# RWKV-7 block on one core: a second ring of four banks in the first half of a section, small roots as powers on GpSimd, and a new order of the steps

## The chip, the cores and the metric

The kernel runs on one core of a Trainium2 chip. The metric is the device time of one execution in microseconds (us), as the median of several runs. The core has five engines that run side by side: TensorE (PE in the profile; PEld is its weight load), VectorE (DVE), ScalarE (ACT), GpSimd (POOL) and SyncE (SP), which here only issues transfers. They meet through semaphores only.

## What is computed

The input x is 2 x 4096 tokens of 256 channels, fp32. After a layer norm it goes through two branches, whose product is added to x:

```python
xn = _layernorm(x)
s = _L0_attn_ref(xn, ...)          # RWKV-7 time mixing, 4 heads of 64
g = _silu(_L0_ffn_ref(xn, ...))    # down(silu(gate(x)) * up(x)), 256 -> 768 -> 256
x = x + s * g
```

In the time mixing, each token is mixed with the one before it by four sets of weights made from a small tanh layer (mix0 to mix3, for wa, k, rg and v). From the mixed inputs come the receptance r, the key k, the value v, the decay w, the rates a and ma, the gate g and the normed key kk. Then runs a recurrence over the tokens of each head:

```python
S = S * dt[:, :, None, :] + sa[..., None] * bt[:, :, None, :] + vt[..., None] * kt[:, :, None, :]
y = jnp.einsum('bhij,bhj->bhi', S, rt)
```

with `sa = S at`, a = -kk, b = kk * a. Its output goes through a group norm over each head, (yh - mu) * rsqrt(var + EPS), gets a bonus term, is multiplied by g and projected by w_output.

## The kernel before

The 4096 tokens of both batches are cut into 16 tiles t of 256 tokens (512 columns with two batches). The recurrence is worked in blocks of 32 tokens: within a block by triangular matrices, from block to block by a state ST, in eight steps c of a tile.

Every engine has its own program, made of the same streams, each a generator that does one step per `yield`. In a *section* up to four tiles are in work at once: L is the input norm of tile i+1; F (mixing), D (decays), K (keys), R (receptance), V (values), E (update) and X (pairs) are the front part of tile i; N (the feed-forward part) and B (back, the recurrence) are for tile i-1; O (output) is for tile i-2. There are 15 sections that hold front and back together.

The order of the steps on an engine is a string, ORDER, with one letter for each step; walk() takes the next step of the stream that the letter names. An engine works its instructions strictly in this order. Written out with step names, PE's first part of a section before is:

```
gate00 gate01 up00 mix0 up01 yT0 yT1 gate02 gate03 up02 up03 out0 mix1 gate04
lora gate05 k0 out1 z gh v0 k1 hk v1 r0 r1 band corner kk vT0 up04 up05 values0
state0 rn vT1 u0 g0 ...
```

gate and up are halves of the feed-forward's products (4 matmul instructions each, since fp32 takes two passes), down and ffn its last product, xT, yT and vT transposes, band and corner the last two products of the inverse of a 32 x 32 triangle, whose 16 x 16 parts VectorE inverts in the steps inv0 to inv14 and flip. values, state, u, s and y are the steps of the recurrence, half, matrix and KT those of the pairs.

PSUM has eight banks. Four of them (`bank`) are a Ring: room() gives the next one and makes PE wait until its last tile has been read. Nearly all products of PE outside the recurrence take one. The other four (`chunk_banks`, also seen as `spare_bank`) belong to the recurrence; in the first half of a section mix0 (L381) and then the first parts of z, na and nma (L397, L400, L406) use them at fixed places, with the signals mix_made, z_made and rates_made. back() has PE wait, ahead of values0, until ScalarE has taken z, na and nma of the next tile.

Lines that matter below: L356 is the matmul of project(), for lora, k, hk, gh, r, v and mixin; L386 mix1; L422 kk and mk; L455 vT; L506 gate and up; L516 down; L535 band and L543 corner; L559 values, L568 outputs, L584 state, L598 u, L612 s; L625 yT; L634 out. On ScalarE L648 is the square root of the input norm and L900 that of the group norm, each followed by a reciprocal on VectorE (L929, L1182); L701 copies k, L820 and L823 are the decays' Exp and Ln, L839 is the Silu of the gate, L680 and L684 the sigmoids, L865 takes y out, L871 band. On VectorE L962 is the mixing, L969 the decays' n, L986 the fl steps, L996 kk. On GpSimd L1246 adds the mixed parts to x, L1272 is mkz, L1282 e3, L1305 fades the state, L1236 moves the last token of a tile.

SyncE's program after a tile's pairs are done is a chain: store and reload the matrices for the inverse, load the residual (`Y<-in_x`), store the inverse, reload it for band, and load its parts into TT ahead of values0.

Of the kernel before, what the change touches and what calls it, by code (L numbers as in the profile page):

```python
# [16 lines left out]
H, N = 4, 64  # L17
# [30 lines left out]
for _n, _w in (("ident", 128), ("bd", 128), ("center", 128), ("am0", 256), ("ti", HL * HL)):  # L48
# [4 lines left out]
ORDER = {"pe": ("NNNFNOONNNNOFNFNKOFRVKKVRRBBKVNNBBKVBVBBVBBBBBNBBBNBBBNBBNBBNEBNNNBBNNBBNNBNBBXXBBNXXXBXBBNBBLBNBBXX"  # L53
            "BBLXXXX"),
         "act": ("ONNNFKFFFOOFFRFDKVKDVBRRBKKKVVBEBKBBBKVBXXBBVDBVBBVNNXBLBBNXBNBBXXLBXBBLLBXBBNXBBLXX"),
         "dve": ("BOFNOONBBBOBFFFFFFFBOBBBBBBBBBBBDDDDDKKDDNKDKDBBBXEBLBEXBXBEXBXEXENXXBXXLXBNXXBXXXXXNBXXXBXXXXXBXXXL"
             "BLXXXBXBX"),
         "pool": ("FFFFFFFFDBFEXEBKBXBBBBBL")}
# [54 lines left out]
def program(nc, d):  # L113
    with ExitStack() as ctx:
# [13 lines left out]
        eps = sb("eps", [128, 4])  # L128
# [41 lines left out]
        qpad = [sb(f"qpad{i}", [128, QC, NJ, 2, 2, BL]) for i in range(2)]  # L170
# [12 lines left out]
        SF = sb("SF", [128, B, NH, N])  # L183
        rhs = sb("rhs", [128, 2, 128])
# [17 lines left out]
        ring = Ring(bank, [semaphore(f"bank_full{i}") for i in range(NB)])  # L202

# [8 lines left out]
        mix_made, z_made, rates_made = signal("mix_made", 4), signal("z_made", NH), signal("rates_made", 2)  # L212
# [36 lines left out]
        NSET = 13  # L249
# [95 lines left out]
        def pe_program():  # L345
# [28 lines left out]
            def mixing(t):  # L374
                pe.wait_ge(*mixh_ready(t))
                if t >= 2:
                    pe.wait_ge(*y_out(t - 2))
                    pe.wait_ge(*st_ready(t - 2))
                for n in range(4):
                    f = MIX[n][0]  # L380
                    pe.matmul(spare_bank[n], w2[32 * f:32 * f + 32, 0:128], small[32 * f:32 * f + 32, :], start=True, stop=True).then_inc(*mix_made.up)  # L381
# [7 lines left out]
                o = room((t, "lora"), lora_ready(t))  # L389
                pe.wait_ge(*moved(t, 2))  # L390
                project(o[0:112, :], wa1, xwa).then_inc(*ring.fill((t, "lora")))
                yield "lora"
                pe.wait_ge(*lora_ready(t))
                pe.wait_ge(*mixed(t, 7))
                two = [room((t, "na"), na_ready(t)), room((t, "nma"), nma_ready(t))]
                for g in range(NH):
                    pe.matmul(spare_bank[g], wa2[32 * g:32 * g + 32, 128 * g:128 * g + 128], sml2[32 * g:32 * g + 32, :],  # L397
                              start=True, stop=False).then_inc(*z_part.up)
                for n, p0 in enumerate((64, 96)):
                    pe.matmul(spare_bank[2 + n], wa2[p0:p0 + 16, 0:128], sml2[p0:p0 + 16, :], start=True, stop=True).then_inc(*rates_made.up)  # L400
# [1087 lines left out]
```

## Time and profile before

| | us |
|---|---|
| median of 3 runs | 1805.75 (1799.24 to 1811.61) |
| the profiled execution | 1809.13 |
| its span, first to last instruction | 1807.7 |
| mean granted TensorE clock | 0.941 of 2.4 GHz |
| DMA engines, mean | 32 GB/s |

The profiled execution lies within the runs. All durations and gaps that the prediction uses are from it; 1.4 us lie outside its span. A page of the profile gives busy time by engine and by group of instructions; a busy PE is not PE at its peak, since matmuls overlap and their ends are modelled. The granted clock is either 1 or 0.5 (2.4 or 1.2 GHz) and a number between is a mean over a stretch. A wait is put down to the one that came last.

### The profile page before, as it was taken

How to read it: one execution, taken by the hardware profiler on the slowest of the kernel's cores; microseconds unless marked ns; L12 is line 12 of the kernel's file. 1: busy time of each engine (PE TensorE's matmuls, PEld its weight loads, DVE VectorE, ACT ScalarE, POOL GpSimd, SP SyncE). 2: the span in 40 equal slices, each digit the busy share in tenths (PEclk: the TensorE clock that was granted, in tenths of full speed). 3: DMA queues.
4: the chain of work that ended last, by engine and by line, in shares of the span. 5: the costliest groups of instructions: out<-in, count | busy, mean ns of one | idle time of the engine just before them, and what ended most of it. 6: DMA issues, size and time to landing. Idle time of an engine off the chain costs nothing.

```text
span 1807.7 us, 47903 instructions
## 1 busy us (share of the span) xinstructions
PE 1625.3 (90%) x20224; PEld 1116.4 (62%) x20224; DVE 1234.1 (68%) x2608; ACT 1207.0 (67%) x2047; POOL 480.0 (27%) x388
## 2 busy tenths in 40 slices
PE   1679999999998999999899999999999999999966
PEld 0255757667575766757576675757667575765745
DVE  3476777677676777767677676777777676776713
ACT  1838758584875858587584958768585875849512
POOL 0414132241313224141332414132241413324000
PEclk9879999999998999999899999999999999999968
DMA  3011020211202021110201112030211203011110
GB/s 132 12 17 31 9 51 14 50 22 30 42 8 51 14 46 25 30 42 6 54 15 40 31 30 42 3 58 14 45 26 30 42 3 58 14 40 19 35 25 25
DMA packets 251430, 57.83 MB, mean 32 GB/s; under 512 B 223696, under 2 KB 250704, under 8 KB 251088
## 3 DMA queue, kind: packets, MB, share of 16 engines
q1 hardware_dynamic: 241936, 41.95, 12.3%
q10 hardware_dynamic: 9280, 12.81, 2.0%
q8 instruction: 160, 2.62, 0.6%
q14 instruction: 54, 0.44, 0.1%
HBM read 36.38 MB, written 18.35 MB: 30 GB/s over the span
## 4 chain that ended last, share of the span: by engine, by line
PE 77%; SPq 6%; DVE 5%; ACT 4%; DMA 4%; issue 3%; POOL 0%; DVEq 0%; ACTq 0%
PE bank L356 16%; PE bank L506 16%; PE bank L516 10%; PE bank L481 7%; DMA Y<-in_x 3%; PE chunk L612 3%; PE chunk L584 3%; PE chunk L559 3%; PE bank L455 3%; PE chunk L568 2%; PE bank L468 2%; PE bank L634 2%; PE bank L461 2%; PE chunk L598 2%; SPq L1342 1%
## 5 line engine op out<-in xcount | busy, mean ns | idle before, releaser
L506 PE MATMUL bank<-xT,wu 128*128 128x256 f32 x768 | 219.8, 423 | 0.0
L506 PE MATMUL bank<-xT,wg 128*128 128x256 f32 x768 | 202.1, 400 | 18.3 <-DVE KS L962 18.3
L1305 POOL TENSOR_TENSOR SF<-ST,CT 128x256 f32<-128x256 f32 x128 | 97.4, 761 | 450.4 <-DVE ST L1168 450.4
L839 ACT ACTIVATE sg<-bank 128x512 f32<-128x512 f32 x96 | 57.1, 595 | 228.9 <-PE bank L506 228.5
L516 PE MATMUL bank<-wd,hT 128*128 128x256 f32 x768 | 186.5, 393 | 0.0
L1246 POOL TENSOR_TENSOR big<-KS,xT 128x512 f32<-128x512 f32 x64 | 75.2, 1197 | 407.1 <-DVE KS L962 407.1
L506 PEld LDWEIGHTS bank<-xT,wg 128*128 128x128 f32 x768 | 142.8, 196 | 60.1 <-DVE KS L962 30.7
L356 PE MATMUL bank<-big,W 128*128 128x512 f32 (+1 forms) x320 | 167.2, 657 | 13.1 <-POOL big L1246 6.5
L506 PEld LDWEIGHTS bank<-xT,wu 128*128 128x128 f32 x768 | 151.3, 209 | 36.6 <-issue 11.4
L516 PEld LDWEIGHTS bank<-wd,hT 128*128 128x128 f32 x768 | 143.2, 193 | 22.0
L356 PE MATMUL bank<-KS,W 128*128 128x512 f32 x320 | 144.2, 597 | 0.0
L1163 DVE COPY VU<-chunk 32x256 f32<-32x256 f32 x128 | 53.4, 417 | 126.4 <-PE chunk L598 125.9
L481 PE MATMUL bank<-qpad,KS 128*64 128x32 f32 x4096 | 134.0, 225 | 4.8 <-DVE KE L1100 4.5
L865 ACT ACTIVATE Y<-chunk 32x256 f32<-32x256 f32 x256 | 96.3, 376 | 62.4 <-PE chunk L568 58.3
L481 PEld LDWEIGHTS bank<-qpad,KS 128*64 128x64 f32 x4096 | 127.0, 140 | 14.3 <-issue 11.8
L969 DVE SCALAR_TENSOR_TENSOR gT<-big,gT 128x1024 f32<-128x1024 f32 x16 | 39.1, 2445 | 118.5 <-ACT big L823 118.5
L356 PEld LDWEIGHTS bank<-big,W 128*128 128x128 f32 (+1 forms) x320 | 62.8, 204 | 84.3 <-issue 61.0
L356 PEld LDWEIGHTS bank<-KS,W 128*128 128x128 f32 x320 | 59.5, 190 | 81.2 <-issue 81.2
L1128 DVE TENSOR_TENSOR hT<-sg,bank 128x512 f32<-128x512 f32 x96 | 65.9, 686 | 52.3 <-PE bank L506 46.0
L1168 DVE TENSOR_TENSOR ST<-SF,chunk 128x256 f32<-128x256 f32 x128 | 53.8, 420 | 61.9 <-PE chunk L612 60.7
L882 ACT ACTIVATE rhs<-chunk 96x256 f32<-96x256 f32 x128 | 48.2, 376 | 71.0 <-PE chunk L584 69.1
L802 ACT ACTIVATE qpad<-big 64x256 f32<-64x256 f32 x256 | 92.0, 406 | 1.6
(161 smaller groups left out, 3559.9 us busy)
## 6 DMA issues: line engine op xcount, KB each, us to landing
smalls<-in_x SPq DMA_DIRECT2D x32, 256.0 KB, 3.0
Y<-in_x SPq DMA_DIRECT2D x32, 256.0 KB, 3.7
out<-fsil ACTq DMA_DIRECT2D x32, 256.0 KB, 2.2
scrA<-AM SPq DMA_DIRECT2D x64, 64.0 KB, 1.9
hat<-scrB SPq DMA_DIRECT2D x32, 128.0 KB, 3.3
hat<-scrF SPq DMA_DIRECT2D x32, 128.0 KB, 3.1
KE<-scrA SPq DMA_DIRECT2D x64, 32.0 KB, 2.3
scrT<-KE SPq DMA_DIRECT2D x16, 128.0 KB, 1.7
```

The source lines that it names most:

```text
L356: m = pe.matmul(o, weights[:, h, :], x[:, h, :], start=(h == 0), stop=(h == NH - 1))
L455: q = pe.matmul(o[:, 128 * n:128 * n + 128], bv[t % 2][:, h, 128 * n:128 * n + 128], center, start=True, stop=True)
L481: q = pe.matmul(oc[:, :, BL * j:BL * j + BL], K[:, 2 * n + b, 64 * j:64 * j + 64], Q[:, 2 * n + b, j, :, :, :].rearrange("p a b e -> p (a ...
L506: q = pe.matmul(o[:, TT_ * n2:TT_ * n2 + TT_], w[:, h, 128 * (n + n2):128 * (n + n2) + 128], x_now[:, h], start=(h == 0), stop=(h == NH - 1))
L516: q = pe.matmul(o[:, 256 * m:256 * m + 256], hT[:, n, 128 * m:128 * m + 128], wd[:, n, :], start=(n == 0), stop=(n == NF - 1))
L559: pe.matmul(RY[g:g + 64, b, 64 * h2:64 * h2 + 64], A[64 * b:64 * b + 32, c, 64 * h:64 * h + 64], V[64 * b:64 * b + 32, c, 64 * h:64 * h + ...
L802: i = act.activation(Q[p0:p0 + 64, :, :, hh, x, :], own[p0:p0 + 64, qs], ACT.Copy)
L839: act.activation(sg[:, :], ring.tile(key)[:, :], ACT.Silu).then_inc(*sg_ready.up)
L865: i = act.activation(by_batch, RY[64 * x + 32:64 * x + 64, :, :].rearrange("p b (g n) -> p b g n", g=NH), ACT.Copy)
L1128: i = dve.tensor_tensor(hT[:, n:n + 2, :], sg[:, :].rearrange("p (n c) -> p n c", n=2), ring.tile(key)[:, :].rearrange("p (n c) -> p n c", ...
L1246: pool.tensor_tensor(columns(dst[:, h, :]), columns(w[:, h, :]), x_now_of(par, h), ALU.add).then_inc(*moved.up)
L1305: pool.tensor_tensor(SF[:, :, :, :], ST[:, :, :, :], fade[:, c].unsqueeze(3).to_broadcast([128, B, NH, N]), ALU.mult).then_inc(*faded.up)
```

## The change

**A second ring.** A Ring `spare` is put over the four banks of the recurrence, with a semaphore for each bank. early_room() takes the next one and waits for its reader, and for the recurrence of two tiles before. mix0's four products, lora, the two parts of z, na0, nma0, k0, k1, hk, gh, r0, r1, v0 and v1 go there; the first ring keeps the rest. The signals mix_made, z_made and rates_made go.

```diff
         ring = Ring(bank, [semaphore(f"bank_full{i}") for i in range(NB)])
+        spare = Ring(spare_bank, [semaphore(f"spare_full{i}") for i in range(len(spare_bank))])
...
+            def early_room(t, key, emptied):
+
+                o, before = spare.take(key, emptied)
+                if before:
+                    pe.wait_ge(*before)
+                if t >= 2:
+                    pe.wait_ge(*y_out(t - 2))
+                    pe.wait_ge(*st_ready(t - 2))
+                return o
...
                 pe.wait_ge(*lora_ready(t))
-                pe.wait_ge(*mixed(t, 7))
+                four = [early_room(t, (t, "z", g), z_ready(t, g + 1)) for g in range(NH)]
+                four += [early_room(t, (t, name), taken(t, 1)) for name, taken in (("na0", na_ready), ("nma0", nma_ready))]
...
                 for h in range(NH):
-                    o = room((t, "k", h), k_ready(t, h + 1))
-                    project(o[:, :], wk[:, :, 128 * h:128 * h + 128], xk).then_inc(*ring.fill((t, "k", h)))
+                    o = early_room(t, (t, "k", h), k_ready(t, h + 1))
+                    project(o, wk[:, :, 128 * h:128 * h + 128], xk).then_inc(*spare.fill((t, "k", h)))
...
                 pe.wait_ge(*t_loaded(t))
                 if t + 1 < NT:
-                    for taken in (z_ready, na_ready, nma_ready):
-                        pe.wait_ge(*taken(t + 1, 2 if taken is z_ready else 1))
+                    for taken in (z_ready, k_ready, hk_ready, gh_ready, r_ready, v_ready):
+                        pe.wait_ge(*taken(t + 1))
+                    for taken in (na_ready, nma_ready):
+                        pe.wait_ge(*taken(t + 1, 1))
```

With four tiles in the ring, the tenth product (nma0) takes the bank that k0 took, k1 that of z0, hk that of z1, gh that of na0, v0 that of nma0, v1 that of k1, r0 that of hk and r1 that of gh.

**Roots.** The square root on ScalarE and the reciprocal on VectorE become an add of the epsilon and a power of -0.5, both on GpSimd, for the input norm (128x4) and the group norm (128x16). The 1/N of the group norm moves into the Square on ScalarE (a scale). They stand in GpSimd's program after state4 and after state7.

```diff
-                act.activation(rstd[:, :], mv[:, :, 1], ACT.Sqrt, bias=eps[:, 0:1]).then_inc(*x_std.up)
...
-                act.activation(st2[:, :], st2[:, :], ACT.Sqrt, bias=eps[:, 1:2], scale=1.0 / N).then_inc(*y_std.up)
...
+                pool.wait_ge(*y_var(t))
+                pool.tensor_scalar(st2[:, :], st2[:, :], GN_EPS, None, ALU.add).then_inc(*y_std.up)
+                pool.wait_ge(*y_std(t))
+                pool.tensor_tensor(st2[:, :], st2[:, :], minus_half.to_broadcast([128, NM * H]), ALU.pow).then_inc(*y_inv.up)
+                yield "root"
```

**The order.** All four strings are new. Written out, PE's section is now:

```
gate00 gate01 yT0 up00 yT1 up01 gate02 gate03 out0 up02 up03 mix0 mix1 gate04 gate05
lora k0 z out1 k1 hk gh v0 kk v1 r0 r1 rn up04 band up05 corner vT0 down0(2 halves)
gate10 values0 state0 gate11 up10 u0 values1 up11 gate12 s0 gate13 state1 vT1 y0 u1 rk
values2 s1 g0 state2 y1 u2 values3 s2 g1 state3 up12 y2 u3 up13 values4 s3 half0 state4
matrix0 y3 u4 gate14 values5 s4 gate15 state5 y4 u5 KT0 values6 s5 up14 state6 half1 y5
u6 matrix1 values7 s6 up15 state7 KT1 xT y6 u7 half2 matrix2 s7 y7 down1 KT2 half3
matrix3 down1 mixin KT3
```

ScalarE from lora to u0: `lora k0 gate04 na0 nma0 z0 z1 na1 nma1 exp k1 hk ln mk0 mk1 gh sqk v0 em r0 band r1 v1 (two output transfers) corner rn_ln rn vT00 vT0 er state0 ek EF es u0`. VectorE: `groupnorm yT0 yT1 up00 unit inv0 inv1 out0 up02 inv2 mix00 ... mix31 inv3 ... inv10 out1 inv11 ... inv14 flip kk0 n nd kk1 cs2 cs4 cs8 rn0 rn1 up04 fl3 fl2 fl1 dm k fl0 b rk qa u0 s0 qa0 ...`. GpSimd: `state0 mix00 ... mix31 mixa zero mkz e3 kem kk qr state1 ... state4 root state5 state6 x0 state7 root`. SyncE's order is the same as before.

**Small.** The constants eps become two columns, 1 and -0.5; two memsets fewer at the start; qpad is declared later, so it lies at another address.

## Rows read from the trace of the kernel before

**Rows 1.** The page's first part: engine, busy us (share of the span), instructions
```profile
PE 1625.3 (90%) x20224; PEld 1116.4 (62%) x20224; DVE 1234.1 (68%) x2608; ACT 1207.0 (67%) x2047; POOL 480.0 (27%) x388
```

**Rows 2.** Busy time by stretch: from:to, length, busy us, PEclk, DMA share, GB/s
```profile
230.00:336.00 106.00, 100.64 (x1272) 69.71 (x1271) 77.50 (x164) 75.46 (x129) 30.09 (x24) 0.97 0.16 33
...
972.00:1078.00 106.00, 99.59 (x1266) 68.29 (x1265) 76.54 (x162) 75.45 (x128) 30.02 (x24) 0.97 0.15 31
...
1502.00:1608.00 106.00, 100.83 (x1264) 69.33 (x1264) 76.29 (x163) 75.43 (x128) 30.07 (x24) 0.95 0.15 30
```

**Rows 3.** The chain that ended last, in order of time: start, us, what
```profile
245.87 12.21 PE bank L356 x28
...
1624.19 12.21 PE bank L356 x28
```

**Rows 4.** Waits of PE: what waited <- for what: total us, times, longest
```profile
PE bank L506 <- DVE KS L962: 18.3, 15, 2.2
PE bank L386 <- DVE fsil L1205: 14.6, 14, 1.4
...
PE bank L455 <- DVE KS L996: 14.0, 16, 1.9
...
PE bank L543 <- ACT hat L871: 12.6, 16, 0.8
```

**Rows 5.** PE alone by stretches of 1 us: length, busy (x), PEclk, DMA share, GB/s
```profile
1109.00:1110.00 1.00, 1.00 (x8) 0.50 0.27 28
...
1115.00:1116.00 1.00, 1.00 (x5) 0.60 0.00 0
...
1293.00:1294.00 1.00, 1.00 (x4) 0.65 0.00 0
```

**Rows 6.** Timeline of PE: start us, us, instruction, count
```profile
1076.23 1.89 PE L506 MATMUL bank<-xT,wu 128*128 128x256 f32 x8
...
1113.57 3.00 PE L506 MATMUL bank<-xT,wu 128*128 128x256 f32 x8
```

**Rows 7.** Timeline of ScalarE about the group norm's root
```profile
1069.72 1.28 ACT L900 ACT_TABLE_LOAD   x1
1071.01 0.31 ACT L900 ACTIVATE st<-st,eps 128x16 f32<-128x16 f32 x1
1071.34 1.28 ACT L839 ACT_TABLE_LOAD   x1
```

**Rows 8.** Groups of instructions: count, busy us, mean ns, idle before
```profile
L839 ACT ACT_TABLE_LOAD x31 | 39.8, 1283 | 0.6
...
L1236 POOL COPY xT<-xT 128x4 f32<-128x4 f32 x16 | 5.9, 371 | 7.1 <-DVE AM L1223 7.1
```

**Rows 9.** Timelines of GpSimd (L1246, L1272, L1282) and VectorE (L969, L986)
```profile
1086.80 4.63 POOL L1246 TENSOR_TENSOR KS<-KS,xT 128x512 f32<-128x512 f32 x4
...
1112.63 2.36 POOL L1272 TENSOR_TENSOR big<-big,gT 128x1024 f32<-128x1024 f32 x1 [6.89 <-ACT big L712]
1114.95 1.89 POOL L1282 TENSOR_TENSOR big<-big 128x1024 f32<-128x1024 f32 x1
...
1104.31 2.51 DVE L969 SCALAR_TENSOR_TENSOR gT<-big,gT 128x1024 f32<-128x1024 f32 x1 [6.71 <-ACT big L823]
...
1112.65 4.31 DVE L986 TENSOR_TENSOR KS<-KS,big 128x32 f32<-128x32 f32 x2
```

**Rows 10.** Timeline of ScalarE: k0's copy, then a sigmoid, load and Exp
```profile
1089.32 0.60 ACT L701 ACTIVATE KB<-bank 128x512 f32<-128x512 f32 x1
...
1096.65 0.74 ACT L684 ACTIVATE big<-bank,nvec 128x512 f32<-128x512 f32 x1
1097.41 1.28 ACT L820 ACT_TABLE_LOAD   x1
1098.70 1.06 ACT L820 ACTIVATE big<-big 128x1024 f32<-128x1024 f32 x1
```

**Rows 11.** Timeline of PE at the end, with the idle time before
```profile
1794.22 1.97 PE L625 MATMUL bank<-con,Y 128*128 128x128 f32 x8 [5.14 <-DVE Y L1184]
```

More of the change, by code:

```diff
@@ L183, in program @@
         SF = sb("SF", [128, B, NH, N])
+        qpad = [sb(f"qpad{i}", [128, QC, NJ, 2, 2, BL]) for i in range(2)]
         rhs = sb("rhs", [128, 2, 128])
@@ L375, in mixing @@
                 pe.wait_ge(*mixh_ready(t))
[L376 to L379, printed above, removed]
+                four = [early_room(t, (t, "mix0", n), mixed(t, 2 * n + 1)) for n in range(4)]
+                for n, o in enumerate(four):
                     f = MIX[n][0]
-                    pe.matmul(spare_bank[n], w2[32 * f:32 * f + 32, 0:128], small[32 * f:32 * f + 32, :], start=True, stop=True).then_inc(*mix_made.up)
+                    pe.matmul(o, w2[32 * f:32 * f + 32, 0:128], small[32 * f:32 * f + 32, :], start=True, stop=True).then_inc(*spare.fill((t, "mix0", n)))
                 yield "mix0"
@@ L728, in receptance @@
                 key = (t, "gh")
-                act.wait_ge(*ring.full(key))
+                act.wait_ge(*spare.full(key))
                 act.wait_ge(*ring.full((t, "nma")))
-                act.wait_ge(*z_made(t))
-                act.activation(sml2[:, :], ring.tile(key)[:, :], ACT.Tanh).then_inc(*gh_ready.up)
+                for g in range(NH):
+                    act.wait_ge(*spare.full((t, "z", g)))
+                act.activation(sml2[:, :], spare.tile(key), ACT.Tanh).then_inc(*gh_ready.up)
                 yield "gh"
-                act.wait_ge(*ring.full((t, "r", NH - 1)))
+                act.wait_ge(*spare.full((t, "r", NH - 1)))
                 for h in range(NH):
-                    act.activation(rT[:, h, :], ring.tile((t, "r", h))[:, :], ACT.Copy).then_inc(*r_ready.up)
+                    act.activation(rT[:, h, :], spare.tile((t, "r", h)), ACT.Copy).then_inc(*r_ready.up)
                     yield f"r{h}"
@@ L744, in value @@
                     key = (t, "v", h)
-                    act.wait_ge(*ring.full(key))
-                    act.activation(bv[par][:, h, :], ring.tile(key)[:, :], ACT.Copy).then_inc(*v_ready.up)
+                    act.wait_ge(*spare.full(key))
+                    act.activation(bv[par][:, h, :], spare.tile(key), ACT.Copy).then_inc(*v_ready.up)
                     yield f"v{h}"
@@ L957, in mixing @@
                         dve.wait_ge(*xx_ready(t, h + 1))
-                    if h == 0:
-                        dve.wait_ge(*mix_made(t))
-                    else:
-                        dve.wait_ge(*ring.full((t, "mix", n)))
-                    dve.scalar_tensor_tensor(out=w[:, h, :], in0=ring.tile((t, "mix", n))[:, :] if h else spare_bank[n], scalar=v(maa, h),
+                    dve.wait_ge(*(ring.full((t, "mix", n)) if h else spare.full((t, "mix0", n))))
+                    dve.scalar_tensor_tensor(out=w[:, h, :], in0=ring.tile((t, "mix", n))[:, :] if h else spare.tile((t, "mix0", n)), scalar=v(maa, h),
                                              in1=xx[:, h, :], op0=ALU.add, op1=ALU.mult).then_inc(*mixed.up)
@@ L1212, in dve_program @@
             n_set = 0
-            for level, col in ((LN_EPS, 0), (GN_EPS, 1), (1.0, 2), (0.0, 3)):
-                dve.memset(eps[:, col:col + 1], level).then_inc(s_set, 1)
+            for level, col in ((1.0, 0), (-0.5, 1)):
+                dve.memset(one[:, col:col + 1], level).then_inc(s_set, 1)
                 n_set += 1
@@ L1252, in decays @@
             def decays(t):
-                pool.wait_ge(*ring.full((t, "v", NH - 1)))
+                pool.wait_ge(*spare.full((t, "v", NH - 1)))
                 pool.memset(FL[:, :, :], 0.0).then_inc(*fl_zero.up)
```

95 lines of the change are left out of this document (46 added, 49 removed).

## Prediction

> **What bounds the kernel now.** I read the page's busy times first: TensorE (PE) is busy 90% of the span, ScalarE 67%, GpSimd 27% [rows 1]. PE's matmuls are the same before and after the change, so the question is what lies between them and at what clock they run. The stretches by section come next [rows 2]. There are thirteen stretches of 106 us between 230 and 1608 us, each as long as a full section; the first, the one with the least work and the last are shown. PE is busy 99.6 to 101.0 us in them, 100.5 in the mean, so 5.5 us are idle, and the mean granted clock is 0.97 in five and 0.95 in eight, 0.958 over all. So PE is at its lower level, 1.2 GHz, for (1 - 0.958) / 0.5 = 8% of the time, 8.9 us of 106. Of these some 1.5 us are idle anyway, and half of the rest, 3.7 us, is what the low clock costs. The chain of what ended last gives the period: its longest piece, 28 matmuls of L356 in a row, stands in it fourteen times, first at 245.87 and last at 1624.19 us, so a section takes 1378.32 / 13 = 106.0 us [rows 3]. A section at full clock and without idle time would take 106.0 - 5.5 - 3.7 = 96.8 us. All that a new order can win is in these 9.2 us, plus the ends of the program.
>
> The waits say who causes the idle time [rows 4]. The gates of L506 wait for the mixing on VectorE (18.3 us in all), mix1 (L386) for a bank that out0 holds (14.6), vT for kk on VectorE (14.0), the corner matmuls (L543) for band's copy on ScalarE (12.6). Nearly all stand in the first half of a section, where every projection takes a bank from one ring of four, while the recurrence's own four banks lie nearly empty. The clock falls just there: at 1109 us, after band, corner and two waits between them, until 1115 us, and in other sections also at 1293 us, behind mix1 [rows 5]. PE was then busy with short, narrow matmuls and gaps. Eight L506 matmuls take 1.89 us at full and 3.00 us at the low clock [rows 6].
>
> **The change, part by part.**
>
> *Roots on GpSimd.* ScalarE loses two square roots a section. The group norm's costs a table load of 1.28 us, and the Silu behind it another [rows 7]; the input norm's root costs a load too. There are 207 loads in the run, 13 a section, of 1283 ns each (L839's 31 stand in [rows 8]). In the new ScalarE order I count 8 changes of table a section: Sigmoid, Exp, Ln, Sigmoid, Exp, Ln, Exp, Silu. That is 6.4 us, and 0.6 us of roots, of some 75 us that ScalarE is busy. VectorE loses two reciprocals of 0.2 us. GpSimd gains four tiny instructions; power isn't in the trace. Its nearest row is a copy of 128x4, 371 ns [rows 8]; as upper bound I take 2.36 us, a 128x1024 add [rows 9]. The group norm's pair stands behind variance, which by the sum below ends 5.7 us before the section does, and yT0 is due 1.7 us after its start. So 0.8 to 4.7 us are hidden; I take 0.8. The input norm's pair has some 3 us of cover. Worth to the path: nothing in itself; it shortens ScalarE's queue.
>
> A table load starts 0.02 us after the last Sigmoid's end, and the Exp 0.01 us after the load [rows 10]. The Trainium skill (ScalarE: Activation LUTs, What ACT_TABLE_LOAD costs) adds a drain of about 1380 ns to each load; by that five loads fewer would be an estimated 13.3 us of ScalarE time, by the rows 6.4. The rows decide.
>
> *The second ring.* mix0, lora, z, na0, nma0, k, hk, gh, r and v move to the recurrence's four banks. PE copies nothing more; it waits for other readers. In return values0 waits until ScalarE has taken all of z, k, hk, gh, r and v of the next tile; in the new order all are taken some 7 us earlier.
>
> *The new order.* I follow a section, time 0 at gate00, with steps at full clock: half a gate or up 0.86 us, projections and out 1.73, half a down 2.79, a recurrence step 0.39, pairs of a quarter 1.99. The dense start (gates, yT, out0, ups) takes 9.5 us with every operand in time, mix0 and mix1 2.0 more: 11.5. Then come these stalls of PE:
> - gate04 needs the bank of mix01, which VectorE frees at 12.3: 0.9 us (before 18.3 / 15 = 1.2).
> - gate04, gate05, lora run to 15.9. k0 needs xk, the fourth add of GpSimd: four of them take 4.63 us [rows 9], from 11.5 to 16.1: 0.3.
> - z needs nma0's bank, which k0 holds; ScalarE copies k0 in 0.60 us [rows 10] plus two handovers: 0.75. This wait is new.
> - k1 needs z0's bank, behind a table load, na0, nma0 and z0 on ScalarE: 0.3.
> - r1 needs gh's bank. ScalarE has to pass, from 18.6 on, z1, na1, nma1, Exp, k1, hk, Ln and the mk pair, with four loads: gh is done at 34.8, PE there at 34.3: 0.5.
> - rn needs the squares of kk. VectorE takes kk1 behind the decays' n, 2.51 us [rows 9], and nd: kk1 ends at 35.5, the squares at 37.5, PE is there at 36.6: 1.05.
> - corner, vT1, u2, s0 and s2: 0.1 to 0.4 each, 1.05 together.
>
> Sum 4.85 us in the first 65 us. In the rest the recurrence has less dense work between its steps; I take 0.9 us, between nothing and the 6.3 of the last rival below. Idle 5.75 us, slightly more than before.
>
> One thing supports itself thinly: on ScalarE everything from k0's copy to u0 (18 to 55 us) is one chain with hardly a gap, and u0's copy ends at 54.9 us, when PE arrives at 55.0. VectorE's u0 stands behind b, rk and qa, which wait for kk on GpSimd, done at 50.3; it ends at 54.3. No slack is left there.
>
> VectorE's inverse steps inv3 to inv10 now lie beside GpSimd's adds. The row shows what happens then: two fl additions took 4.31 us together, until GpSimd's two instructions of 2.36 and 1.89 us were over [rows 9]. The Trainium skill (SBUF — State Buffer, SBUF: two separate sides) calls the pair of ports that both share an exclusive lock, and the trace agrees. Sixteen instructions of 0.24 us would by the row end at 23.7 us instead of 20.8; out1 comes at 22.6 and what follows needs the flip only by 39.5 us less the 7.5 us of loads. By row or rule, this costs PE nothing.
>
> *Clock.* Where the low clock came before, PE now mixes dense steps in: gate halves between band and corner, two downs behind them, vT after them. The narrow stretches are shorter, but z with its wait (3 us) and rn, band, corner with theirs remain. Bounds: 0, or 3.7 us as before. I take 1.0, since part of a low stretch would fall into waits for ScalarE.
>
> Period: the same matmuls, 96.8 by the difference above; my sum from the steps is 94.3 us, and before it lacked some 1.9 us of small overheads (drains ahead of a wait, mostly), 96.2. With 96.2 + 5.75 + 1.0 = 103.0 us a section wins 3.0 us, times 15 = 45 us.
>
> *Ends.* In the last sections PE idles on the recurrence's tail: 5.14 us in front of the last yT [rows 11]. The new order puts all of down1 (5.6 us) behind y7 and down0 in front of values0, where PE waited for loads, and one table load leaves the last chain. 8 us, between 0 and 14. The prologue I take as unchanged, as I do qpad's new address and two memsets fewer.
>
> Sum: 1807.7 - 45 - 8 = 1755 us of span, against an execution that took 1809.1 with a median of 1805.75: the median to expect is **1753 us**.
>
> **The rivals.**
> - *The clock never falls* and idle time stays at 4.6: period 101, 15 x 5 + 8 = 83 us, 1723. For it: dense steps stand in every narrow stretch. Against it: z.
> - *The clock falls once a section as before*: 3 us instead of 1, less shadow: period 105 to 104.9, 15 + 8 = 23 us, 1783. For it: PE has as much idle time as before.
> - *The second ring only moves the waits.* ScalarE's chain from k0 to u0 is 2 us longer than I sum, at no slack: period 105 plus a low stretch, near 106, and of the ends' 8 us some 6 remain: 1800.
> - *The recurrence becomes the bound* (the slower side). Steps 1 to 7 are now only 3.3 to 6 us apart on PE, with copies on VectorE and ScalarE behind instructions of up to 1.2 us. If each of the seven waits 0.9 us, that is 6.3 us, 5.4 more than counted: 15 x (103.0 + 5.4 - 106.0) = 36 us over before with nothing won at the ends, 1842. It decides from some 0.55 us a step on, where 3.0 + 0.9 us are used up by seven. For it: less dense work is left there to cover a copy. Against it: ScalarE has fewer table loads to run between two steps.
>
> **How the numbers follow.** Forecast (1740 to 1770) 0.35, clock never falls 0.22, falls as before 0.20, waits only moved 0.12, recurrence bound 0.11. The range 1715 to 1800 leaves out the last and the lower part of the second. A measurement tells about 1% from no change, 18 us: faster is below 1788. The first three lie there, 0.77 less a rest of the third: 0.76. Same 0.13, slower 0.11.
>
> **What would show it.** Right: 8 table loads a section; a wait of z for ScalarE's k0; a wait of rn; yT0 without wait; idle time of 5 to 6 us, mean clock 0.98 or more. Wrong: a clock of 0.95; waits of u, s or state steps over 0.5 us each; a GpSimd power of over 4 us, which would show before groupnorm.

## The result and the profile after

Measured beside the kernel before, medians of four runs each (for before, the three runs told above and one more):

| kernel | median us | lowest to highest | ratio to before | 95% interval |
|---|---|---|---|---|
| before | 1808.34 | 1799.24 to 1811.61 | 1 | |
| after | 1724.39 | 1710.04 to 1724.95 | 0.9524 | 0.9463 to 0.9586 |

The profiled execution of after took 1724.95 us, its span 1723.5 (before 1807.7). The span lost 84.2 us, 4.7%. The forecast was 53 us.

The page's first part after, to lay beside [rows 1]:

```profile
PE 1580.1 (92%) x20224; PEld 1088.6 (63%) x20224; DVE 1256.4 (73%) x2574; ACT 1099.9 (64%) x1937; POOL 538.1 (31%) x452
```

PE works the same 20224 matmuls in 45 us less busy time: their clock has risen, the mean granted clock of the execution from 0.941 to 0.973. The other 39 us of the span are idle time of PE. ScalarE has lost 107 us of work, GpSimd has gained 58.

Where along the span did it go? The band matmuls (L535 before, L546 after) mark each section. First, last but one and last of each kernel, timelines of PE, start and length in us:

```profile
154.45 1.15 PE L535 MATMUL bank<-hat 64*64 64x64 f32 x32
...
1636.33 1.15 PE L535 MATMUL bank<-hat 64*64 64x64 f32 x32
...
1729.27 1.97 PE L535 MATMUL bank<-hat 64*64 64x64 f32 x32 [14.11 <-issue]
```

```profile
150.60 1.15 PE L546 MATMUL bank<-hat 64*64 64x64 f32 x32
...
1561.73 1.15 PE L546 MATMUL bank<-hat 64*64 64x64 f32 x32
...
1644.94 1.97 PE L546 MATMUL bank<-hat 64*64 64x64 f32 x32 [11.56 <-issue]
```

The front won 3.85 us. Fourteen intervals won 1481.88 - 1411.13 = 70.75, that is 5.05 us each (from 105.85 to 100.80 us). The last interval won 9.73 (92.94 to 83.21), and the tail behind the last band lost 0.2 (78.4 to 78.6).

What a full section is made of shows best in stretches cut at the section's own marks (the start of down's 24 matmuls of L527 in the chain, of L356's 28 before). Columns: from:to, length, then busy us of PE, PEld, DVE, ACT, POOL, granted clock, DMA share, GB/s. Two sections of before, one with the least and one with a typical amount of low clock:

```profile
989.49:1093.23 103.74, 97.94 (x1266) 67.75 (x1265) 76.64 (x163) 75.45 (x129) 30.02 (x24) 0.98 0.15 32
1197.97:1304.00 106.03, 100.88 (x1265) 69.19 (x1265) 76.61 (x163) 75.43 (x129) 29.97 (x24) 0.95 0.15 31
```

Two of after:

```profile
1159.13:1259.44 100.31, 96.26 (x1265) 66.50 (x1265) 78.06 (x161) 68.57 (x122) 33.46 (x28) 1.00 0.16 33
1259.44:1361.60 102.16, 97.91 (x1266) 67.17 (x1265) 77.91 (x161) 68.70 (x122) 34.18 (x28) 0.98 0.16 32
```

A section's matmuls at full clock take 96.3 us: the first row of after shows it, with 1265 matmuls at clock 1.00. What PE is busy above that is the price of the low clock. Before, it was 1.7 us in the first of the two rows, 4.6 in the second, up to 5.8 in others (102.1 us busy), and by the mean of [rows 2] 100.5 - 96.3 = 4.2. After, ten of the thirteen sections between 255 and 1566 us last 100.3 to 100.6 us, 100.4 in the mean, and the last three 102.0 to 102.5, as in the second row, with 1.65 us of low clock: 0.4 in the mean. Over all fourteen intervals from band to band, the mean busy time of PE went from 100.3 to 96.7 us and its idle time from 5.6 to 4.1. So of the 5.05 us, 3.6 are clock and 1.4 idle time. (Fifteen times 3.6 is 54 us, more than the 45 that PE's busy time lost in all: the tail gives some back, as will be seen.)

Where the clock still falls, it is behind z, one of the places named in advance. PE alone by stretches of 1 us, in the section that starts at 1315 us, where z had waited 1.44 us until 1335.44:

```profile
1336.00:1337.00 1.00, 1.00 (x14) 0.95 0.05 16
1337.00:1338.00 1.00, 1.00 (x8) 0.50 0.00 0
...
1340.00:1341.00 1.00, 1.00 (x6) 0.84 0.00 0
```

The waits of PE after, against [rows 4]:

```profile
PE chunk L407 <- ACT KB L711: 20.1, 16, 1.4
PE bank L517 <- DVE KS L965: 13.1, 15, 0.9
...
PE bank L500 <- ACT sg L850: 9.2, 14, 0.7
PE bank L441 <- ACT KS L728: 8.5, 16, 0.6
```

L407 is z waiting for ScalarE's copy of k0 (new, 1.26 us a section), L517 gate04 (0.87), L500 KT3 (0.66), L441 rn (0.56). The waits of mix1, vT and corner that stood in every section are gone.

### The profile page after: what moved, and what is told of

The parts are those of the page before. It is cut to its first block, busy times and chain, and to the rows that moved or that the text cites. A ratio compares the mean times of both kernels' runs of the same rounds, so it can differ in the third digit from the quotient of the medians.

```text
span 1723.5 us, 48139 instructions
## 1 busy us (share of the span) xinstructions
PE 1580.1 (92%) x20224; PEld 1088.6 (63%) x20224; DVE 1256.4 (73%) x2574; ACT 1099.9 (64%) x1937; POOL 538.1 (31%) x452
## 4 chain that ended last, share of the span: by engine, by line
PE 73%; DVE 9%; ACT 7%; issue 4%; POOL 4%; SPq 2%; DMA 2%; DVEq 0%; ACTq 0%; POOLq 0%
PE bank L517 18%; PE bank L527 9%; PE chunk L367 9%; PE bank L492 6%; POOL big L1252 3%; PE bank L647 3%; PE chunk L597 3%; PE chunk L625 3%; PE chunk L572 3%; PE bank L466 2%; PE bank L479 2%; PE bank L472 2%; PE chunk L581 2%; PE bank L500 2%; ACT Y L876 2%
## 5 line engine op out<-in xcount | busy, mean ns | idle before, releaser
L517 PE MATMUL bank<-xT,wg 128*128 128x256 f32 x768 | 199.5, 392 | 13.7 <-DVE KS L965 13.1
L517 PE MATMUL bank<-xT,wu 128*128 128x256 f32 x768 | 210.8, 400 | 0.0
L1311 POOL TENSOR_TENSOR SF<-ST,CT 128x256 f32<-128x256 f32 x128 | 81.9, 639 | 329.3 <-DVE ST L1171 329.2
L527 PE MATMUL bank<-wd,hT 128*128 128x256 f32 x768 | 180.7, 390 | 0.0
L517 PEld LDWEIGHTS bank<-xT,wg 128*128 128x128 f32 x768 | 138.5, 190 | 46.6 <-DVE KS L965 25.5
L527 PEld LDWEIGHTS bank<-wd,hT 128*128 128x128 f32 x768 | 144.9, 194 | 20.3
L517 PEld LDWEIGHTS bank<-xT,wu 128*128 128x128 f32 x768 | 136.4, 192 | 32.6 <-issue 12.2
L492 PE MATMUL bank<-qpad,KS 128*64 128x32 f32 x4096 | 139.8, 225 | 8.2 <-DVE KE L1103 8.2
L367 PE MATMUL chunk<-KS,W 128*128 128x512 f32 x320 | 144.6, 598 | 0.0
L367 PE MATMUL chunk<-big,W 128*112 128x512 f32 (+1 forms) x256 | 119.5, 600 | 6.7 <-ACT gT L702 3.0
L367 PEld LDWEIGHTS chunk<-KS,W 128*128 128x128 f32 x320 | 59.2, 190 | 81.9 <-issue 75.0
L850 ACT ACTIVATE sg<-bank 128x512 f32<-128x512 f32 x96 | 57.2, 595 | 82.4 <-DVE hT L1131 58.2
L682 ACT ACTIVATE smalls<-chunk 64x512 f32<-64x512 f32 x16 | 9.5, 591 | 148.7 <-PE chunk L367 148.7
L1152 DVE SCALAR_TENSOR_TENSOR KE<-KE 128x15 f32<-128x15 f32 (+7 forms) x240 | 89.9, 375 | 9.5 <-DMA KE<-scrA 1.7
```

Source lines behind the costliest of these rows:

```text
L492: q = pe.matmul(oc[:, :, BL * j:BL * j + BL], K[:, 2 * n + b, 64 * j:64 * j + 64], Q[:, 2 * n + b, j, :, :, :].rearrange("p a b e -> p (a ...
L517: q = pe.matmul(o[:, TT_ * n2:TT_ * n2 + TT_], w[:, h, 128 * (n + n2):128 * (n + n2) + 128], x_now[:, h], start=(h == 0), stop=(h == NH - 1))
L527: q = pe.matmul(o[:, 256 * m:256 * m + 256], hT[:, n, 128 * m:128 * m + 128], wd[:, n, :], start=(n == 0), stop=(n == NF - 1))
L850: act.activation(sg[:, :], ring.tile(key)[:, :], ACT.Silu).then_inc(*sg_ready.up)
L1152: dve.scalar_tensor_tensor(out=pv, in0=TL[:, 0:nj, s:s + 1].to_broadcast([128, nj, w]), scalar=1.0, in1=AL[:, s, s + 1:HL].unsqueeze(1).to ...
L1311: pool.tensor_tensor(SF[:, :, :, :], ST[:, :, :, :], fade[:, c].unsqueeze(3).to_broadcast([128, B, NH, N]), ALU.mult).then_inc(*faded.up)
```

## The experiments

The question: three parts were changed together. Which of them carries the gain, and through what? My first theory was that the order makes the gain, the ring only allows it, and the roots are worth nothing. The rivals: the roots carry a part through ScalarE's table loads, or the ring alone removes the waits. On the clock, the theory was that dense steps mixed into narrow ones keep it up; the rival, that the shorter waits do. One combination wasn't tried: the new order with only one ring. By the orders on paper its products would wait for banks whose readers stand behind later products, a wait in a circle; so what the ring is worth could be measured only with the old order.

All ratios are against the kernel before on the same chip, with 95% intervals. Kernels start from after, where nothing else is said. Stretches and waits are those of each kernel's one profiled execution. The line numbers of a step shift by a few from kernel to kernel; the text names the step.

### Single parts and pairs

**Ring and roots, but the old order.** PE's string as before the change; the others too, apart from the two roots' new places.

```diff
-"pe": ("NNONONNNONNFFNNFKFOKKRVKVRRKNBNBVNNNBBNNBBNNBNBV...
+"pe": ("NNNFNOONNNNOFNFNKOFRVKKVRRBBKVNNBBKVBVBBVBBBBBN...
```

> The kernel after with the four orders of before (the small roots placed as after has them). Theory A, the order makes the gain and the second ring only allows it: 1785 to 1808 us, the granted clock falls in every section as before (mean about 0.95), PE idle 5 us of a section. Theory B, the second ring itself removes waits for banks: 1745 us or less.

**The new order and the ring, but the roots on ScalarE and VectorE again.** The core of the edit (both roots alike):

```diff
+                act.activation(st2[:, :], st2[:, :], ACT.Sqrt, bias=eps[:, 1:2], scale=1.0 / N).then_inc(*y_std.up)
+                dve.reciprocal(st2[:, :], st2[:, :]).then_inc(*y_inv.up)
-                pool.tensor_scalar(st2[:, :], st2[:, :], GN_EPS, None, ALU.add).then_inc(*y_std.up)
-                pool.tensor_tensor(st2[:, :], st2[:, :], minus_half.to_broadcast([128, NM * H]), ALU.pow).then_inc(*y_inv.up)
```

> The kernel after with the two square roots back on ScalarE and the reciprocals on VectorE, at the places in the order that they had before. Theory A: ScalarE has idle time at the section's start (it waits 9.4 us for lora there), so the table loads of the group norm's root cost nothing, and the input norm's falls into the second half: 1724 to 1740 us, clock 0.97. Theory C, relieving ScalarE is what pays: 5 loads are 6.4 us a section, up to 15 x 6.4 = 96 us, 1780 us or more.

**Before plus the roots on GpSimd alone** (the reverse of the edit just shown):

> The kernel before with the roots moved to GpSimd and nothing else. Theory A: 1795 to 1808 us, the same waits of PE and the same clock. Theory C: 1760 us or less.

**Before plus the second ring alone** (the ring's part of the change's diff, and nothing else):

> The kernel before with the second ring and nothing else: old orders, old roots. Theory A: 1795 to 1812 us; the waits of gate04 for mix01, of mix1 for out0 and of vT0 for kk stay, since they are not for the banks that the ring adds. Theory B: 1760 us or less.

Measured:

| ring | roots on GpSimd | new order | median us | ratio to before |
|---|---|---|---|---|
| yes | yes | no | 1832.0 | 1.0159 (1.0110 to 1.0209) |
| yes | no | yes | 1826.1 | 1.0107 (1.0057 to 1.0156) |
| no | yes | no | 1810.6 | 1.0036 (1.0015 to 1.0058) |
| yes | no | no | 1827.6 | 1.0128 (1.0092 to 1.0164) |
| yes | yes | yes (after) | 1724.4 | 0.9524 (0.9463 to 0.9586) |

Neither of the two parts tried alone wins anything, nor does either pair; the three together win 4.8%. The ring by itself costs 23 us. Its largest new wait of PE is one row:

```profile
PE chunk L364 <- ACT gT L702: 21.9, 16, 1.4
```

In the old order gh's product comes straight behind z, and with four tiles in the ring it takes the bank of z0, whose readers (L702 is the Relu) ScalarE reaches late: 1.4 us, sixteen times. That isn't yet the loss: from band to band PE idles 7.3 us instead of 5.6, but is busy 1.05 us less, since less of the section passes at the low clock, so the period is only 0.7 us longer (106.56). Another 5.8 us lie ahead of the first band; why is open. The row is the same in the kernel with ring and roots and the old order (`L365 <- ACT gT L700`). The roots with the old order do nothing but shorten ScalarE's queue (70.9 us busy a section instead of 75.4): its waits stay nearly as they were, and so does the time, within half a percent. So far the theory holds.

It falls with the second kernel. With the new order and the ring kept, moving the roots back loses all of the gain and 1% more, where my expectation was 1724 to 1740 us. Its waits of PE:

```profile
PE bank L635 <- DVE Y L1192: 36.4, 16, 3.9
...
PE bank L497 <- ACT sg L850: 27.2, 14, 2.0
PE chunk L404 <- ACT KB L711: 19.9, 16, 1.4
PE chunk L569 <- ACT Y L876: 17.3, 33, 1.0
```

They are yT, KT3, z and values. The first hardly existed after (0.3 us in all), the second was 9.2, the fourth 6.2; z's is as before the edit. The timelines of ScalarE, then PE, at the turn of a section show why:

```profile
979.00 0.59 ACT L825 ACTIVATE KT<-bank 128x512 f32<-128x512 f32 x1
979.61 1.28 ACT L911 ACT_TABLE_LOAD   x1
980.90 0.31 ACT L911 ACTIVATE st<-st,eps 128x16 f32<-128x16 f32 x1
...
982.81 0.66 PE L635 MATMUL bank<-con,Y 128*128 128x128 f32 x4 [2.17 <-DVE Y L1192]
```

ScalarE comes to the group norm's root only behind KT3's copy, and pays a load for it. yT0, which the new order puts right behind the section's first two gate halves, waits 2.17 us for Y. On GpSimd the root is done by then. The other root loads its table in the middle of the recurrence, and delays ScalarE's Silus and copies there.

This kernel also answers the question on the clock in part. PE's order is after's, matmul for matmul, and still the low clock is back: from band to band (108.9 us) PE idles 8.4 us, 4.2 more than after, and is busy 100.5 us, 3.8 more. It doesn't fall at rn, band and corner, where the dense steps stand, but nearly always right behind the new waits, of KT3 (until 962.52 us) and of yT (until 982.81). PE by stretches of 1 us:

```profile
963.00:964.00 1.00, 1.00 (x8) 0.60 0.00 0
...
984.00:985.00 1.00, 1.00 (x4) 0.50 0.42 95
```

So the order alone doesn't keep the clock up; it needs the short waits as well.

### Each root by itself

**Only the group norm's root back on ScalarE:**

> The kernel after with only the group norm's root back on ScalarE and VectorE. e2 showed yT0 waiting 2 us for the scaled Y. Theory F, the chain variance, root, yT0 is what the new order can't wait for (it has yT0 one step after the section's start): the wait of yT comes back, 1760 to 1800 us. Theory G, the harm in e2 came from the input norm's root and its two table loads in the second half: 1725 to 1740 us.

**Only the input norm's root back:**

> The kernel after with only the input norm's root back on ScalarE, with the reciprocal on VectorE. With both roots back the kernel took 1826 us, with the group norm's alone 1777. If the two add up, this one gives 1724 + 49 = 1770 us, with waits of KT3 for the late Silu (27 us in all in the kernel with both). If they need each other: 1725 to 1740 us.

Measured 1777.0 us, 0.9851 (0.9820 to 0.9882), and 1767.2 us, 0.9778 (0.9729 to 0.9826). Against after's ratio of 0.9524 that is some 59 and 46 us. The wait of yT is whole in the first of them (`L636 <- DVE Y L1188: 36.5`) and missing in the second; the wait of KT3 is the other way round, 9.0 us in the first, as after, and in the second:

```profile
PE bank L498 <- ACT sg L851: 27.2, 14, 2.0
```

So each root has a wait of its own, and the two losses add up to nearly that of both: 59 + 46 = 105 us, and 105 by the ratio of the kernel with both back. Each kernel has sections with the clock at 1.00 throughout (102.72 and 102.54 us; after's take 100.31), and others of 104 to 107 us. In both, 2.1 to 2.2 us a section are idle time more than after, and the rest of the loss is low clock. The stretch of each:

```profile
1091.56:1194.28 102.72, 96.49 (x1265) 66.43 (x1265) 78.35 (x162) 71.44 (x125) 30.31 (x26) 1.00 0.16 32
```

```profile
987.93:1090.47 102.54, 96.38 (x1265) 66.49 (x1265) 78.19 (x162) 71.44 (x125) 32.18 (x26) 1.00 0.16 32
```

**Root on ScalarE, but what needs it later.** If yT's place is what makes the group norm's root dear, then putting yT0 and yT1 behind up01 on PE, and up00 ahead of yT0 on VectorE, should give back most of it:

```diff
-PE  NNONONNNO   gate00 gate01 yT0 up00 yT1 up01 gate02 gate03 out0
+PE  NNNNOONNO   gate00 gate01 up00 up01 yT0 yT1 gate02 gate03 out0
-DVE OOONB       groupnorm yT0 yT1 up00 unit
+DVE ONOOB       groupnorm up00 yT0 yT1 unit
```

> As the kernel with the group norm's root back (1777 us), but PE does yT0 and yT1 behind up01, 1.7 us later, and VectorE up00 ahead of yT0. Theory F, the root's chain is late only because the new order has yT0 so early: the wait of 2.2 us of yT falls below 0.6 us, 1730 to 1750 us. If it is the table loads themselves that hurt: no change, 1777 us.

Measured 1756.3 us, 0.9719 (0.9682 to 0.9756): by the ratios 24 of the 59 us came back, less than expected. The wait of yT fell from 36.5 to 10.5, but a part of it moved one step on, to out0:

```profile
PE bank L645 <- DVE hat L1201: 23.7, 16, 2.6
```

A section with the clock at 1.00 still takes 102.66 us, as without the edit (102.72). What was won is mostly clock: eleven of the fourteen intervals are of that kind, where it was eight. This later place of yT doesn't cover a root on ScalarE; an earlier place of the root in ScalarE's own order wasn't tried.

### The dense steps in the narrow stretch

**Narrow steps side by side.** rn, band, corner and vT0 in a row, up04 and up05 behind them; everything else as after. Written with step names:

```diff
-rn up04 band up05 corner vT0
+rn band corner vT0 up04 up05
```

> The kernel after with four steps of PE moved: rn, band, corner, vT0 stand side by side again, up04 and up05 behind them. Theory A, the clock stays up because dense matmuls stand between the narrow ones: now corner waits some 0.8 us for band's copy and the low clock returns behind it in most sections, 1 to 3.5 us a section, 1745 to 1785 us, mean clock 0.95 to 0.96. Theory D, the clock is up only because less time is idle in all: 1725 to 1740 us, clock 0.97.

**The opposite in the kernel before:** its own band and corner pulled apart by up04 and up05, and VectorE's up04 put ahead of kk0; no ring, roots on ScalarE:

```diff
-band corner kk vT0 up04 up05 values0
+up04 band up05 corner kk vT0 values0
```

> The kernel before, one ring and old roots, with one thing changed: up04 and up05 of PE stand around band instead of behind vT0 (and VectorE's up04 ahead of kk0, so that its bank comes free). Theory A, the clock alone is worth about 3 us a section and dense steps keep it up: 1755 to 1780 us, the waits for band's copy and the fall of the clock at band and corner gone. Theory D: 1800 us or more.

**Filler in the kernel before.** Matmuls whose result nobody reads, added in front of corner, kk and vT0, into a bank that is free then. They are dense (128 rows, 128 columns of weights, 256 columns each). The kernel does more work, and computes the same:

```diff
+            def filler(n):
+                for _ in range(n):
+                    pe.matmul(spare_bank[3][:, 0:256], wg[:, 0, 0:128], wg[:, 0, 0:256], start=True, stop=True)
```

> The kernel before with work added: where PE waits in the first half of a section, it first does dense 128x128x256 matmuls on weights, whose result nobody reads: two ahead of corner (0.86 us in a wait of 0.79), one ahead of kk (0.43 in 0.46), two ahead of vT0 (0.86 in 0.78). Theory A, the low clock by itself costs 3 to 4 us a section and comes from these waits: the fall behind corner goes, a section loses 2 to 3 us less by it and gains at most 0.4 us of work: 1765 to 1785 us with more work done. Theory D, the clock is not what sets the period: 1805 to 1815 us.

| kernel | median us | ratio to before |
|---|---|---|
| after, narrow steps together | 1772.9 | 0.9853 (0.9798 to 0.9908) |
| before, ups between | 1830.6 | 1.0154 (1.0117 to 1.0191) |
| before, filler | 1792.1 | 0.9941 (0.9904 to 0.9977) |

Put side by side, the narrow steps lose more than half of the gain. But for the larger part it isn't the clock. Its stretches, a section without and one with low clock:

```profile
470.29:573.16 102.87, 96.05 (x1265) 66.72 (x1265) 79.22 (x161) 68.47 (x122) 34.21 (x28) 1.00 0.15 32
573.16:677.62 104.46, 97.65 (x1265) 67.62 (x1265) 79.25 (x161) 70.07 (x124) 34.34 (x29) 0.98 0.16 32
```

Even at full clock the section is 2.5 us longer than after's, all of it idle time: corner now waits 1.90 us for ScalarE's copy of band, and down waits 0.9 us for the last up:

```profile
PE bank L552 <- ACT hat L880: 29.3, 16, 1.9
...
PE bank L525 <- DVE hT L1129: 13.6, 16, 0.9
```

The low clock adds 1.6 us, and only in five of the fourteen intervals from band to band; at 1086 to 1090 us, in this narrow stretch. So up04 and up05 between the narrow steps are worth 2.5 us as cover for ScalarE's copies, and some 0.6 us on average as a support of the clock. (That is in an execution with a mean clock of 0.970; the others had 0.960 to 0.972, so it may be somewhat more.)

The opposite edit on before lost 1.5%: corner's wait went, but values0 lost the cover of its transfer:

```profile
PE chunk L557 <- DMA TT<-scrU: 25.4, 15, 5.3
```

The clock still fell in that part of the section: over 1010 to 1030 us it is 0.83, behind waits of 0.85 us (kk), 0.83 (vT0) and 1.18 (values0). Two dense steps alone neither keep the clock nor win time with these waits beside them. In after, down0 and gate10 stand ahead of values0, and it has no such wait.

The filler is the direct test of the clock. Each section has ten matmul instructions more, 2.7 us of them by the stretches below (99.00 - 96.3), and yet takes less time: 104.9 us in the mean of the fourteen intervals, against 105.85. (The first, with 17 us at the low clock, takes 111.2; without it, it is 104.45 against 106.0.) Stretches:

```profile
989.04:1092.64 103.60, 99.00 (x1276) 68.02 (x1275) 76.35 (x163) 75.46 (x129) 29.97 (x24) 1.00 0.15 32
1092.64:1197.55 104.91, 100.48 (x1276) 68.84 (x1275) 76.36 (x163) 75.46 (x129) 29.92 (x24) 0.98 0.15 31
```

In the first the clock never falls; in the second it does, between 1187 and 1190 us, behind mix1 and gate04 with waits of 1.02 and 0.87 us, where no filler stands. PE's busy time is hardly more than before's (97.94 and 100.88), with 2.7 us more to do: the low clock costs 0 and 1.5 us in these two sections, 1.7 and 4.6 in those. Over the fourteen intervals it costs 1.4 us instead of 4.0, and idle time is 1.0 less, as part of the filler fills waits; with 2.7 us more work 0.9 us a section is left as gain. Without the 2.6 us of clock the kernel would be slower than before. In seven executions the mean clock was 0.956 to 0.974, in ten of before beside them 0.934 to 0.948. So the low clock is a price of its own, which work that nobody needs can lower. The gain of 13.5 us is less than the 20 to 40 expected: one low stretch stayed, and the filler takes time of its own.

### The one new wait

**z ahead of k0.** z waits 1.26 us for k0's copy. With z before k0 on PE (and nma0, z0, z1 ahead of k0 on ScalarE, as the ring asks for it) this wait has no cause.

```diff
-PE  gate04 gate05 lora k0 z out1 k1 hk
+PE  gate04 lora gate05 z out1 k0 k1 hk
-ACT lora k0 gate04 na0 nma0 z0 z1 na1 nma1 exp k1 hk
+ACT lora gate04 na0 nma0 z0 z1 k0 na1 nma1 exp k1 hk
```

> The kernel after with z ahead of k0: PE goes gate04, lora, gate05, z, out1, k0, and ScalarE copies k0 after z1. nma0 then takes lora's bank, so z waits for lora's copies alone. Theory A, the 1.26 us wait of z for k0's copy is on the path: it goes, some 0.4 us of waits for lora come, 1708 to 1720 us. Theory E, what follows on ScalarE is the bound anyway and the wait moves to rn or u0: 1722 to 1727 us.

Measured 1719.2 us, 0.9530 (0.9498 to 0.9561). By its ratio it can't be told from after. The wait has changed its cause, not gone. PE's timeline there:

```profile
1028.29 1.13 PE L515 MATMUL bank<-xT,wg 128*128 128x256 f32 x4 [0.88 <-DVE KS L963]
1029.90 1.94 PE L365 MATMUL chunk<-big,W 128*112 128x512 f32 x4 [0.47 <-POOL big L1250]
1033.64 0.70 PE L405 MATMUL chunk<-smalls,W 32*128 32x512 f32 x2 [0.93 <-ACT smalls L681]
```

lora now waits for GpSimd's fourth add, and z for ScalarE's reading of lora: 0.47 + 0.93 in place of 1.26. What differs is the clock: all fourteen intervals take 100.3 to 100.5 us, and the last three, which in after took 102.0 to 102.5, do too. The period is that of after at full clock, so 100.3 us is what this order gives on this kernel; the 5 us between the profiled spans (1718.3 and 1723.5) are mainly those three sections.

## Why the prediction was right, and where it was short

The direction held, the median lies inside the range, and the gain was 31 us larger than forecast. By the prediction's own sum (15 sections and the ends):

| term | forecast us | measured us | from |
|---|---|---|---|
| a section's own matmuls | 96.2 to 96.8 | 96.3 | stretch at clock 1.00 |
| idle time in a section | 5.75 | 4.1 in the mean | stretches |
| low clock in a section | 1.0 | near 0 in ten, 1.65 in three | stretches |
| period | 103.0 | 100.8 | band to band |
| period before | 106.0 | 105.85 | band to band |
| won in 15 sections | 45 | 76 | 15 x 5.05 |
| ends | 8 | 8.4 | 84.2 - 15 x 5.05 |

**What bounds the kernel.** Right: 9.2 us a section were to be won at most between PE's matmuls and in their clock, 5.05 were. The estimate for the low clock, 3.7, was a little low (4.2); the idle time of 5.5 stands, and with it the 96.8 becomes 96.3.

**Idle time: the step list.** A section of after, at 914 us, stall by stall:

| stall of PE | forecast | measured |
|---|---|---|
| gate04 for mix01 | 0.9 | 0.87 |
| k0 for the fourth add | 0.3 | 0 |
| z for k0's copy (new) | 0.75 | 1.26 |
| k1, r1 | 0.3 + 0.5 | 0 |
| rn for the squares | 1.05 | 0.56 |
| corner, vT1, u2, s0, s2 | 1.05 | 0 |
| the rest of the section | 0.9 | 1.28 |
| sum | 5.75 | 3.97 |

The rows for it, from PE's timeline, are these:

```profile
926.66 2.00 PE L517 MATMUL bank<-xT,wg 128*128 128x256 f32 x8 [0.87 <-DVE KS L965]
928.50 3.97 PE L367 MATMUL chunk<-big,W 128*112 128x512 f32 x8
933.72 0.70 PE L407 MATMUL chunk<-smalls,W 32*128 32x512 f32 x2 [1.26 <-ACT KB L711]
...
951.81 1.09 PE L441 MATMUL bank<-KS,con 64*64 64x512 f32 x8 [0.56 <-ACT KS L728]
952.83 1.13 PE L517 MATMUL bank<-xT,wu 128*128 128x256 f32 x4
953.89 1.15 PE L546 MATMUL bank<-hat 64*64 64x64 f32 x32
```

The three that were worked out from a named reader with a duration in the rows came, at 0.87, 1.26 and 0.56. The failed ones were those where I took PE to arrive with no margin and added a few tenths for the handover; a margin of zero by hand was a small margin in truth. Of the signs named in advance, the one of 5 to 6 us of idle time didn't come. rn is half of the forecast; kk1's forerunner, the decays' n, took 1.22 us (from 946.63) and not 2.51. In [rows 9] it ran beside a GpSimd instruction of 2.36 us that began at 1103.38; after, GpSimd was idle there. z is longer because of the handovers: k0's copy starts 0.1 us behind the product and takes 0.60 us (932.56 to 933.16), and z starts 0.56 us behind its end, where I had put 0.15 for both handovers.

**The clock.** Of the 2.2 us by which the period came out shorter than forecast, 1.6 are idle time and 0.6 are clock: I took 1.0 us for it, 0.4 in the mean were lost, and I gave the case that it never falls 0.22. It never fell in ten sections of thirteen. The place where it falls in the other three, behind z and its wait, was the one I had against it. Over the stretches that the forecast went by, the clock gave back 3.8 us a section (4.2 to 0.4) where 2.7 were counted. That the mixed dense steps buy it was only a part of the mechanism: with PE's order kept and the roots back, all of it is lost, so it takes the short waits as well. In the end the time, 1724, is that of the rival "the clock never falls" (1723), though its idle time was to be 4.6: a little more idle time was won, a little less clock.

**The roots.** The prediction said they were worth "to the path: nothing in itself". That holds for before (1.0036) and fails for after, where by the ratios 59 and 46 us hang on them, more together than the whole gain. So the change is faster for a reason that the forecast didn't have: by its reckoning the new order and the ring would have won nearly the same without the roots, and that kernel lost 1%. That the roots were in the change is luck, as far as the forecast goes. The step that failed is that I costed the roots on GpSimd against the section's end, and never asked what a root on ScalarE would do in the new order: yT0 moved to 1.7 us behind the section's start, and KT3's and the Silus' margin in the second half went to almost nothing (0.66 us of wait even so). Their own size was right only in its bounds; 0.8 us was taken. Timeline of GpSimd:

```profile
909.22 0.26 POOL L1315 TENSOR_SCALAR st<-st 128x16 f32<-128x16 f32 x1 [9.95 <-DVE st L1178]
909.57 2.92 POOL L1317 TENSOR_TENSOR st<-st,one 128x16 f32<-128x16 f32 x1
```

The pair takes 3.2 us, within the 4.7 of the upper bound. It starts 4.8 us before the section does (forecast 5.7), and yT0 has no wait.

The number of table loads came as counted, eight a section. ScalarE's load again starts right behind the instruction ahead and the next one right behind the load (979.61, 980.90 in the rows above). The Trainium skill (ScalarE: Activation LUTs, What ACT_TABLE_LOAD costs) would add a drain of about 1380 ns to each; no gap of that kind is in the rows, before or after.

**The second ring.** Its costs were taken as other waits' causes only, and that was right for z. That it loses 23 us without the new order was not said, as the forecast never priced the parts alone.

**VectorE's inverse steps beside GpSimd's adds** cost PE nothing, as forecast. VectorE's timeline:

```profile
931.59 1.20 DVE L1156 SCALAR_TENSOR_TENSOR KE<-KE 128x48 f32<-128x48 f32 x1
...
939.63 0.21 DVE L1156 SCALAR_TENSOR_TENSOR KE<-KE 128x48 f32<-128x48 f32 x1
939.87 2.31 DVE L1152 SCALAR_TENSOR_TENSOR KE<-KE 128x39 f32<-128x39 f32 x1
...
943.33 0.38 DVE L1161 COPY KE<-KE 64x256 f32<-64x256 f32 x1
```

The same instruction on the same shape takes 1.20 us beside a GpSimd add and 0.21 without one, and one of 39 columns lasts 2.31 us beside a GpSimd instruction of 2.36. But only some are caught so, and the last is done at 943.3.

**The ends** gave 8.4 us, as forecast, but elsewhere, so that the number fits is luck: 3.85 in the prologue, which I took as unchanged, 4.7 in the last interval beyond a section's share, and nothing in the tail, where I had looked for it. There PE's idle time in front of the last yT went from 5.14 us [rows 11] to 0.30, but the stretch before it runs at the lower level, 1.2 GHz. The same distance from the end, after and before:

```profile
1680.00:1690.00 10.00, 9.69 (x153) 7.03 (x150) 2.10 (x5) 2.77 (x8) 0.62 (x1) 0.50 0.01 3
1690.00:1700.00 10.00, 8.94 (x141) 6.35 (x144) 2.20 (x5) 3.61 (x9) 1.24 (x2) 0.50 0.01 2
```

```profile
1765.00:1775.00 10.00, 8.99 (x169) 6.57 (x168) 1.89 (x5) 3.61 (x9) 0.62 (x1) 1.00 0.02 4
1775.00:1785.00 10.00, 8.31 (x114) 6.53 (x115) 1.82 (x4) 1.89 (x5) 1.25 (x2) 0.83 0.01 2
```

Behind the last band PE idles 10.9 us instead of 20.2, and is busy 67.7 instead of 58.2. So the idle time that the tail lost came back as slower matmuls. That the dense work, all done by then, leaves narrow matmuls alone there is my reading of it; what the tail would take with dense filler in it wasn't tried.

**What stays open.** Why the clock falls in the last three sections of after and not in the ten before, with the same order, isn't settled; z ahead of k0 had no such section in its profile, but by its median it isn't told from after. Most of the low clock that is left lies at the ends: of some 93 us at 1.2 GHz in the profiled execution of after (a mean clock of 0.973), 10 are in those three sections. The execution at 0.984, which took 1710.04 us, had some 55 by the same sum, so most of what it gained must be at the ends too; no trace shows it. And how the clock's gain divides between the place of the dense steps and the shorter waits is known only at the points measured: 0.6 us a section for up04 and up05, 3.8 us with both roots back.

## What to carry to other kernels

Price an edit in the order that it will stand in, not in the one it is taken from: here ring and roots alone, and both pairs that can be run, lose or win nothing, and all three together win 4.8%. The traces show why for the roots: on GpSimd they take away the waits of yT and KT3 that the new order runs into; and the order takes away gh's wait that the ring runs into. When TensorE is over 90% busy, look at the granted clock before looking for shorter work: in this kernel 3.6 of 5.05 us a section came back as clock, with the same matmuls, and went again when two waits of 2 us returned. And a dense step between narrow ones is worth most as cover for the copy on another engine that the next narrow one waits for; look which transfer or copy loses its cover when it is taken from elsewhere.

## What was not expected of the hardware

- Adding 2.7 us of unread matmuls to each section of the kernel before made it faster by 0.6% (ratio 0.9904 to 0.9977), with a mean granted clock of 0.956 to 0.974 over whole executions, where it had been 0.934 to 0.948.
- A power on GpSimd takes 2.92 us for 128x16 elements and 1.04 us for 128x4, against 0.26 us for an add of the 128x16. From these two points, an estimate is 0.16 us for each column more.
- TensorE's clock fell to 1.2 GHz behind idle times of 0.88 and 1.44 us (from 1318 us on), while PE was 100% busy by the rows (1336 to 1341 us of after), and it didn't fall in the same place of ten sections before that.
